# Value products two groups of four heads behind the scores instead of one, in a two-layer attention and expert kernel

## The reference, cut to what matters

```python
w = jnp.einsum('bhqd,bhkd->bhqk', q, k) / jnp.sqrt(jnp.asarray(HD, q.dtype))
w = jnp.where(mask, w, neg)            # causal; tril with k=2 in the cross attention
w = jax.nn.softmax(w, axis=-1)
a = jnp.einsum('bhqk,bhkd->bhqd', w, v)
```

## Time and profile before

| | |
|---|---|
| median of three runs | 1644.99 us |
| the profiled execution, its own time | 1647.01 us |
| its span, first to last instruction | 1645.3 us |
| TensorE matmuls busy | 1434.1 us, 87% of the span |
| VectorE busy | 1116.3 us, 68% |
| ScalarE busy | 987.8 us, 60% |
| GpSimd busy | 317.8 us, 19% |
| L1394, value products | 4096 matmuls |
| L711, exponentials | 512, 406.0 us |
| L1025, maxima | 1024, 508.6 us |
| mean granted TensorE clock | 0.954 of full speed |

### The profile page before, as it was taken

How to read it: one execution, slowest core, us unless ns; L and a number is a source line. 1 busy time by engine, 2 the same in 40 slices (tenths; PEclk the granted TensorE clock), 3 DMA queues, 4 the chain that set the end, 5 groups by cost and what they waited for, 6 DMA issues and landing times. The chain is left out here.

```text
span 1645.3 us, 39092 instructions
## 1 busy us (share of the span) xinstructions
PE 1434.1 (87%) x15448; PEld 877.4 (53%) x15448; DVE 1116.3 (68%) x3252; ACT 987.8 (60%) x1618; POOL 317.8 (19%) x428
## 2 busy tenths in 40 slices
PE   2667789989898989989898998989899898989887
PEld 1445564655555565655556465555646565555443
DVE  5557676767777776776777676677767667647344
ACT  2255675766757576675757576575757666571642
POOL 3421121211212121121212111121212112020120
PEclk7679999999999999999999999999999999998898
DMA  3334212122040402213040212204031211010000
GB/s 69 57 77 52 55 22 55 21 44 38 22 59 9 67 15 39 36 32 50 10 72 10 50 26 39 43 16 64 10 56 20 44 32 28 9 24 12 15 5 9
DMA packets 79214, 58.05 MB, mean 35 GB/s; under 512 B 11004, under 2 KB 78902, under 8 KB 79030
## 3 DMA queue, kind: packets, MB, share of 16 engines
q1 hardware_dynamic: 76726, 53.90, 18.8%
q10 hardware_dynamic: 2304, 1.64, 0.7%
HBM read 11.57 MB, written 4.19 MB: 10 GB/s over the span
## 5 line engine op out<-in xcount | busy, mean ns | idle before, releaser
L1025 DVE TENSOR_REDUCE chunkmax<-ps 128x3 f32<-128x384 f32 (+1 forms) x1024 | 508.6, 553 | 119.2 <-PE ps L1379 113.6
L711 ACT ACTIVATE probs<-ps 128x768 f32<-128x768 f32 (+1 forms) x512 | 406.0, 809 | 199.3 <-PE ps L1374 195.5
L1444 PE MATMUL ps<-zT,w 128*128 128x512 f32 x576 | 281.0, 602 | 6.5 <-ACT silu_a L728 4.8
L728 ACT ACTIVATE silu_a<-ps,b 128x512 f32<-128x512 f32 x144 | 98.7, 685 | 197.9 <-PE ps L1444 174.5
L1359 PE MATMUL ps<-k_op,q_op 48*128 48x256 bf16 x512 | 147.4, 290 | 64.4 <-DVE chunkmax L1025 50.8
L1166 DVE SCALAR_TENSOR_TENSOR h_open<-ps,b,silu_a 128x512 f32<-128x512 f32 x128 | 95.8, 749 | 123.6 <-PE ps L1444 111.3
L1444 PEld LDWEIGHTS ps<-zT,w 128*128 128x128 f32 x576 | 102.8, 191 | 114.6 <-issue 87.4
L1341 PE MATMUL ps<-q_op,k_op 51*128 51x256 bf16 x512 | 141.7, 277 | 25.2 <-POOL lower L499 9.3
L1480 PE MATMUL ps<-hT,w 128*128 128x512 f32 x288 | 149.3, 599 | 3.8 <-DVE hT L1172 3.0
L1359 PE MATMUL ps<-xk_op,xq_op 51*128 51x256 bf16 x512 | 143.5, 282 | 6.1 <-DVE chunkmax L1025 5.7
L1371 PE MATMUL ps<-mask_q_lo,ident_lo 64*128 64x256 bf16 x512 | 145.9, 288 | 0.0
(11 more groups left out here) (245 smaller groups left out, 3436.9 us busy)
## 6 DMA issues: line engine op xcount, KB each, us to landing
q_op<-q_parts SPq DMA_DIRECT2D x192, 64.0 KB
xq_op<-xq_parts SPq DMA_DIRECT2D x192, 64.0 KB
k_op<-k_parts SPq DMA_DIRECT2D x168, 64.0 KB
x_tm<-in_L_attn_hidden_states SPq DMA_DIRECT2D x16, 256.0 KB, 5.9
x_keep<-in_L_attn_hidden_states SPq DMA_DIRECT2D x16, 256.0 KB, 6.1
out<-o_tm SPq DMA_DIRECT2D x16, 256.0 KB, 2.3
k_op<-k_parts ACTq DMA_DIRECT2D x24, 64.0 KB
w<-in_L_ffn_rw SPq DMA_DIRECT2D x1, 1024.0 KB
```

The source lines that it names most:

```text
L711: act.activation(probs[:, four % 2, 2 * pair:2 * pair + 2, 0:T + a.seen], ps[:, 2 * (1 - g % 2):2 * (1 - g % 2) + 2, 0:T + a.seen], ACT.Ex ...
L1025: dve.tensor_reduce(chunkmax[:, b, at, :], ps[:, MAX_BANK[n], 0:3 * a.seen].rearrange("p (c n) -> p c n", c=3), AX.X, ALU.max).then_inc(a. ...
L1444: pe.matmul(ps[:, bank, :], w, src[:], start=True, stop=True).then_inc(sig.sem, 1)
```

## The change

The value products of a group of four heads are issued one block of four steps later, so the order on TensorE becomes

```diff
-        wxq0 = sb("wxq0", [128, D])
         wxq = sb("wxq", [128, D])
-        wxkv = sb("wxkv", [128, 2 * D])
-        wxk = sb("wxk", [128, D])
...
-        probs = sb("probs", [128, 2, 4, T + XW])
+        probs = sb("probs", [128, 3, 4, T + XW])
...
         geluT = sb("geluT", [128, NC, NT])
+        wxq0, wxk, wxkv = geluT[:, 3, 0:D], geluT[:, 3, D:2 * D], geluT[:, 3, 2 * D:4 * D]
...
-        MAX_BANK = [(6, 7, 5)[n % 3] for n in range(20)] + [(6, 7)[n % 2] for n in range(20, 24)] \
-            + [(4, 6, 7)[n % 3] for n in range(24, 2 * H)]
+        MAX_BANK = [(6, 7, 5)[n % 3] for n in range(24)] + [(6, 7)[n % 2] for n in range(24, 28)] \
+            + [(4, 6, 7)[n % 3] for n in range(28, 2 * H)]
...
                 for g in range(first, last):
                     four, pair = divmod(g, 2)
-                    act.wait_ge(*(a.pv.part(j, four - 1) if four >= 2 else used_before))
+                    act.wait_ge(*(a.pv.part(j, four - 2) if four >= 3 else used_before))
                     act.wait_ge(*a.st_ps.part(j, g + 1))
-                    act.activation(probs[:, four % 2, 2 * pair:2 * pair + 2, 0:T + a.seen],
+                    act.activation(probs[:, four % 3, 2 * pair:2 * pair + 2, 0:T + a.seen],
                                    ps[:, 2 * (1 - g % 2):2 * (1 - g % 2) + 2, 0:T + a.seen], ACT.Exp).then_inc(a.exp.sem, 1)
-                    if g == 10:
+                    if g == 11:
                         context_copy(a, 0, j)
...
-                                         probs[:, four % 2, jj, (0 if half else a.seen):(a.seen if half else a.seen + T)],
+                                         probs[:, four % 3, jj, (0 if half else a.seen):(a.seen if half else a.seen + T)],
...
-                    if exists(j) and four:
-                        if four == 1:
+                    if exists(j) and four >= 2:
+                        if four == 2:
                             free_4()
-                        if four == 5:
+                        if four == 6:
                             free_5()
                             if exists(jo):
                                 pe.wait_ge(*other.s_max.part(jo, LAST_IN_5 + 1))
-                        value_group(a, four - 1, j, par)
+                        value_group(a, four - 2, j, par)
                 if exists(j):
+                    value_group(a, 6, j, par)
                     value_group(a, 7, j, par)
```

## The result

The changed kernel takes 1657.53 us (median of five runs, 1655.88 to 1662.42), the kernel before 1646.26 in the same comparison. The ratio is 1.0077, with a 95% interval of 1.0056 to 1.0099: slower, by 0.8% in this ratio; the two medians lie 11.3 us apart. The profiled execution took 1655.88, 8.9 more than that of before.

A forecast was written before the change was run, and what follows sets the result against it. TensorE's list, with matmuls busy 87% of the span, was taken as the bound. 14 self phases x 0.60 = 8.4, 13 cross phases x 0.23 = 3.0 and 1.0 gave 12.4 us more: median 1657, range 1648 to 1666.5.

The forecast's parts named there:

- Self phase, front: Without VG0 ahead of it, step 10 still starts when it did; its wait grows from 0.62 to some 1.4 us.
- Self phase, end: Three value groups instead of two after step 31: the transposes come 0.60 us later in each self phase.
- My lower bound of 0.4: Low bound in us for the self phase's end, if the groups follow each other 0.07 closer.
- Cross phase: Waits before steps 11 (0.81 to 1.6 us) and 19 end unchanged; the copy delays the end 0.23; the extra group is free.
- every wait: Claim that the two phase timelines show all TensorE waits: two listed in the self phase, four in the cross phase.
- its cover: The 1.17 us idle before VG7 in the cross phase hides the extra group (0.79); without it, the cost would be 0.6.
- Bank rotation, third buffer, weights: The two-bank stall moves four steps later, once a phase; the third buffer and weights inside `geluT` change nothing.
- The last two cross phases: They have no query steps; a self phase's cost less the small wait, 0.5 us each, 1.0 together.
- My second rival: The 1.6 us wait before step 11 lowers the clock in cross phases: up to 16 us more, near 1672; chance 0.10.
- my signs of being wrong: Step 10 or 11 released earlier, cross phase under 25.5, self phases at 22.0, or lower clock after either step's wait.
- My price of 1.25: Cost in us of a clock fall in one cross phase, 26.77 less 25.52, up to 13 times.
- the first cross phase: Less interleaved work and no such early wait, so the group is only moved: 0.

The follow-up runs named there:

- experiment 3: The changed kernel with VG0 put back behind step 7, VG1 to VG7 still two blocks behind: 1655.70 us, ratio 1.0052 to the kernel before.
- 7: The changed kernel with ScalarE's `mlp_input` behind exponential 3 of the self phase instead of behind 2: 1645.78 us, ratio 0.9995 to the kernel before.
- experiment 6: The changed kernel with ScalarE's normalisation of a later pair's input behind exponential 15 of the cross phase: 1646.05 us, ratio 0.9991 to the kernel before.
- experiment 1: The kernel before with only the third buffer of exponentials and the three weights inside `geluT`: 1647.24 us, ratio 0.9998.
- experiment 9: The kernel before with `mlp_input` behind exponential 3, the later pair's normalisation behind exponential 15, and VG3 ahead of step 19 in cross phases: 1624.58 us, ratio 0.9849.
- experiment 4: The kernel before with VG3 ahead of step 19 instead of behind it, in both kinds of phase: 1648.23 us, ratio 1.0002.

## Why the prediction was right

The forecast was 1657 within 1648 to 1666, and slower at 0.80. The time is 1657.5. The mechanism was right; that the number agrees to 0.5 us is luck, as the terms show:

- **Self phase, front: right.** Step 10 did not move, and the wait grew in place of the group that had covered it, to 1.25 and not 1.4. Experiments 3 and 7 show the cause from both sides.
- **Self phase, end: right in kind, too large.** I had 0.60 a phase and the trace has 0.31. The spacing of 0.79 is that from a group to transposes. Between two groups it is less: 48 matmuls take 2.16 us, so with 0.86 for the last the first two take 0.65 each. Three groups and the way to the transposes are 2 x 0.65 + 0.79 = 2.09. And the wait before VG7 in the earlier trace rows was not the 0.12 that I read there: from VG6 to the transposes are 1.77 us, so from VG6 to VG7 0.98, where 0.65 would do. The third group filled these 0.33 and so cost half of itself. My lower bound of 0.4 was above the truth as well. I had no row with two groups back to back, and should have let the bound reach further down.
- **Cross phase: right.** The two VectorE waits ended when they did; the first was 1.28, where I had 1.6. The timeline has two more waits that I left out when I wrote of "every wait", 0.61 and 0.29 in the first 4 us of the phase; they stand ahead of all that moves and are the same after. The end moved by the copy, 0.19 against 0.23 (read from the timeline; no run moves the copy alone), and the group was free in the hole before VG7. I had called that hole its cover; experiment 6 prices the cover.
- **Bank rotation, third buffer, weights: right.** The stall moved by four steps with its size; memory costs nothing (experiment 1).
- **The last two cross phases: 0.5 each.** The trace gives 0.53 for the first, and 0.90 for the second at a mean clock of 0.83 instead of 0.91.
- **The clock: mechanism underrated, price overrated.** My second rival said that the wait before step 11 might bring the lower level. It did, after an idle of 1.28 already, and the lower level behind the wait before step 10 or 11 was among my signs of being wrong. In the phase at 701.19 the clock is at 0.50 from just behind that wait; the rows show the wait, the stretch, and what is left of the wait before step 19:

```profile
708.87 0.28 PE L1357 MATMUL ps<-k_op,q_op 48*128 48x256 bf16 x1 [1.28 <-DVE chunkmax L1023]
...
709.80:713.20 3.40, 3.40 (x48) 2.26 (x44) 2.10 (x5) 1.25 (x3) 3.23 (x3) 0.50 0.02 7
...
715.72 0.28 PE L1357 MATMUL ps<-k_op,q_op 48*128 48x256 bf16 x1 [0.57 <-DVE chunkmax L1023]
```

  But it cost nothing there: the phase took 25.70, as at full speed, because the work that it held up ends inside the wait before step 19, which had room (0.57 left of 1.95). The five early falls made phases of 25.70 to 26.02, so 0 to 0.3 us each. A fall behind step 19 costs 1.3 to 1.4 (27.04 to 27.15, less 25.71). In a self phase, with no wait behind it, it cost 1.5, once (23.81 less 22.32). My price of 1.25 for each was that of the wrong place. What a fall costs depends on the stretch behind the wait.
  The rule that I cited beside this rival (the Trainium skill, TensorE: Matmul & The Clock Gate, section A second HAM failure mode) warns that frequent short idles between groups of matmuls can send the clock back and forth. Here the trace agrees: the wait of 1.28 was followed by 0.50 in six of fourteen cross phases and that of 1.25 in one of thirteen self phases, where in the kernel before 0.81 was not in any of fourteen. The length of the one wait does not settle it, though: in experiment 9 the clock fell in three cross phases 4.4 us after their start, ahead of the wait before step 11, with idles of 0.61 and 0.29 in the phase so far. One of the three, in the phase from 411.76:

```profile
416.20:419.60 3.40, 3.40 (x42) 2.00 (x43) 3.14 (x15) 2.35 (x5) 0.55 (x1) 0.50 0.02 5
```

So the total agrees better than its terms. All 17 self phases together are 4.6 us longer in the profile, all 16 cross phases 3.9, and the rest about 0.4, which is the 8.9 of the profiled executions. The sum had 8.4 + 3.0 + 1.0 = 12.4. The overcharge in the self phases (14 x 0.29 = 4) is the larger error. The cross phases agree (3.9 against 4.0) by two errors that cancel: those of turns 3 to 14 are only 0.8 longer together, where 12 x 0.19 would be 2.3, since four falls instead of eight came late; and the first cross phase, which I had put at nothing, is 1.5 longer (22.2 to 23.7), with a fall behind its wait of 1.28. What closes the 3.5 between the 12.4 and the 8.9 is which executions were profiled: that of the kernel before was 2.0 above its median of three, that of the changed kernel 1.6 below its median of five. The two slowest of the five (1662.42 and 1661.16) show a lower mean clock, 0.947 and 0.948 against 0.950, so the falls of the executions differ; in which phases is not on record.

## What to carry to other kernels

A block of work that waits for nothing is filler, and it is worth what it hides. Moving it later leaves every wait between its old and its new place open, and in these runs it paid only where it had covered little before and met a wait at its new place. Before moving it, list the waits of one phase in order, and ask for each whether its end depends on the filler; where it doesn't, the filler ahead of it was free. The cheaper cure can be on the engine that is waited for. Here its last normalisation, moved behind the exponentials, gave 0.5% on the kernel before, and `mlp_input` 0.8% on the changed one, where no order of the matmuls alone was faster than the kernel before.

## What I had not expected of the hardware

- Two groups of 16 float32 matmuls follow each other in 0.65 us, while the way from a group to transposes is 0.79, and one alone lasts 0.86.
- At the lower clock level a cross phase can be as fast as at the upper one (25.70 at a mean clock of 0.93, 25.71 at 1.00). In such a case the mean clock says little of the time until one knows which stretch it fell in.
- A wait reduced from 1.95 to 1.06 (experiment 4) did not keep the clock up: the phase at 321.04 has a mean of 0.93. Another 0.32 of idle, for a maximum, stood 0.9 us behind it. Lengthening the same wait to 2.49 (experiment 3) gave nine late falls where there had been eight, which is no clear difference; but they cost 1.4 us each, where those of before cost 0.5 to 1.3.
